# Moving the last softmax-denominator round of each head behind the V transposes' copies

## The chip, the cores and the metric

The kernel runs as one program on all 8 cores of a Trainium2 chip. Every core holds the full weights and works on its own half of the rows of one of the four batch entries, so the cores compute the same amount and exchange nothing. The metric is the device time of one launch in microseconds, that of the slowest core.

## The reference

One transformer layer with the layernorm on both sides of each block, for x of shape 4 x 2048 x 2048, in float32:

```python
def layer(x):
    x = x + _layernorm(attn(_layernorm(x)))          # 16 heads of 128, softmax over 2048 keys
    x = x + _layernorm(ffn(_layernorm(x)))           # silu(x Wg) * (x Wu), then Wd; hidden 8192
    return x

def attn(x):
    q, k, v = (x @ w_q.T), (x @ w_k.T), (x @ w_v.T)  # reshaped to heads
    p = softmax(einsum('bqhd,bkhd->bhqk', q, k) / sqrt(128))
    return einsum('bhqk,bkhd->bqhd', p, v).reshape(B, S, D) @ w_o.T
```

A core computes the attention output for 1,024 queries against all 2,048 keys, and the feed-forward block for the same 1,024 rows.

## The kernel before

The program is a list of operations for each engine, in program order, with semaphores between the engines. An engine runs its list strictly in that order; an operation whose semaphore is not there yet holds up everything behind it on that engine. The stages are A and B (layernorm, transposes, Q of all heads), C (attention, head by head), D (output projection, two layernorms), E (gate and up) and F (down, last layernorm and output).

The change lies in stage C, in the loop over the 16 heads `h` (lines 413 to 530). Of one head, scores are computed transposed: 16 chunks of 128 keys by 1,024 queries. A chunk is two matmuls into PSUM (`emit_scores_tc`, L426) and one exponential on ScalarE to bf16 (L435). The exponentials are grouped in four rounds of four chunks, which share one buffer `PTR`. Of each round two things are made:

- the product with V, 8 matmuls on TensorE that accumulate in PSUM (`emit_pv_round`, L448);
- the sum over the four chunks, on VectorE in bf16 (`emit_tree_round`): L459 and L464 add two pairs, L469 adds the sums, L477 adds that to the running denominator `RB` (L475 is a copy in its place in round 0). The last of the four operations raises `vsm`.

Between the chunks TensorE has "filler": the K and V projections of the next head in eight groups of 16 matmuls (`emit_kv_group`, L354), evacuated by ScalarE (L371). At the end of the head come the last V product, then `emit_vt`, 16 matmuls against the identity that transpose the next head's V into PSUM (L386), and `emit_vt_copies`, two VectorE copies of the result to SBUF (L398). The first score matmuls of the next head wait for these copies (`vVt`), because they write the same PSUM.

Then the denominator is summed over the partitions: two matmuls of an all-ones matrix with `RB` (L515, called the ones matmuls here), which wait for `vsm` at 4h + 4. VectorE takes the reciprocal of their result (L523, raises `vRc`) and multiplies the head's output with it (L527, raises `vO`). The ones matmuls write the PSUM banks that the K groups use. So the first filler group of a head waits for the reciprocal of the head before:

```python
            if h >= 2 and g < 2:
                w("t", vRc, h - 1)      # h here is the head whose K is projected
```

In the loop over heads that means: in heads 1 to 14, TensorE issues score chunks 0 and 1 and then waits for the reciprocal of the previous head before filler group 0. Head 15 has no filler; its first V product (L448) waits for `vO` of head 14.

The order in VectorE's list around the end of head h, before the change, is: round 3 of the sum (four operations), copy 0, copy 1, reciprocal, multiplication. In TensorE's list it is: V product of round 3, the 16 transposes, the wait for `vsm`, the two ones matmuls, scores 0 and 1 of the next head, filler 0. In ScalarE's list the first exponential of the next head also waits for `vsm` at 4h + 4, since it overwrites `PTR`.

Of the kernel before, what the change touches and what calls it, by code (L numbers as in the profile page):

```python
# [77 lines left out]
def build_nc():  # L78
# [23 lines left out]
    def Bv(off, dims, parts=128):  # L102
        return bass.AP(ABF, off, [[ABF_N, parts]] + [list(d) for d in dims])
# [4 lines left out]
    def Pv(off, dims, parts=128):  # L108
        return bass.AP(PS, off, [[4096, parts]] + [list(d) for d in dims])
# [58 lines left out]
    def op(e, f, ride=None):  # L168
        pair = None
        if ride is not None:  # L170
            c, k = ride
            c.n += k
            pair = (c.s, k)
        if pair is None:
            ops[e].append(f)
        else:
            def g(eng, f=f, pair=pair):
                f(eng).then_inc(*pair)
            ops[e].append(g)

    def w(e, c, v=None):
        if v is None:
            c, v = c
        ops[e].append(lambda eng, s=c.s, v=v: eng.wait_ge(s, v))
# [191 lines left out]
    def emit_vt(h):  # L376
        for r in range(2):
            w("t", kv_evac[("V", h, 2 * r + 1)])
            if r == 0 and h == 0:
                w("t", vA, 16)  # L380
            if r == 0 and h >= 1:
                w("t", sE, 16 * h)
            for i in range(8):
                tcv = r * 8 + i
                ride = (tVt, 1) if i == 7 else None
                op("t", lambda e, tcv=tcv, r=r, i=i: e.matmul(  # L386
                    Pv(r * 1024 + i * 128, [(1, 128)]),
                    Bv(VFM + tcv * 128, [(1, 128)]),
                    Bv(IDENT, [(1, 128)]),
                    start=True, stop=True), ride)  # L390
            vt_mm[(h, r)] = (tVt, tVt.n)

    def emit_vt_copies(h):
        for r in range(2):
            w("v", vt_mm[(h, r)])
            if h >= 1 and r == 0:
                w("v", tRd, 4 * h)
            op("v", lambda e, r=r: e.tensor_copy(  # L398
                Bv(VTM + r * 1024, [(1, 1024)]),
                Pv(r * 1024, [(1, 1024)])), (vVt, 1))  # L400
# [12 lines left out]
    for h in range(H):  # L413

        def emit_scores_tc(tc, h=h):
            pair = tc % 2
            if tc == 0:
                w("t", kv_evac[("K", h, 3)])
                w("t", vVt, 2 * h + 1)
            elif tc == 1:  # L420
                w("t", vVt, 2 * h + 2)
            else:
                w("t", sE, 16 * h + tc - 1)
            for half in range(2):
                ride = (tS, 1) if half == 1 else None
                op("t", lambda e, tc=tc, half=half, pair=pair, h=h: e.matmul(  # L426
                    Pv(pair * 1024 + half * 512, [(1, 512)]),
                    Bv(KSB + (h % 2) * 2048 + tc * 128, [(1, 128)]),
                    Bv(QF + h * 1024 + half * 512, [(1, 512)]),
                    start=True, stop=True), ride)  # L430
            r = tc // 4
            w("s", tS, 16 * h + tc + 1)
            w("s", tRd, 4 * h + r)
            w("s", vsm, 4 * h + r)
            op("s", lambda e, tc=tc, pair=pair: e.activation(  # L435
                Bv(PTR + (tc % 4) * 1024, [(1, 1024)]),
                Pv(pair * 1024, [(1, 1024)]),
                AF.Exp, bias=Fv(ST + 41, [(1, 1)]), scale=QK), (sE, 1))

        def emit_pv_round(r, h=h):  # L440
            w("t", sE, 16 * h + 4 * (r + 1))
            if r == 0:
                w("t", vO, h)
            for i in range(4):
                tcv = 4 * r + i
                for half in range(2):
                    ride = (tRd, 1) if (i == 3 and half == 1) else None
                    op("t", lambda e, tcv=tcv, i=i, half=half, r=r: e.matmul(  # L448
                        Pv(3072 + half * 512, [(1, 512)]),
                        Bv(VTM + tcv * 128, [(1, 128)]),  # L450
                        Bv(PTR + i * 1024 + half * 512, [(1, 512)]),
                        start=(r == 0 and i == 0), stop=(r == 3 and i == 3)), ride)

        def emit_tree_round(r, h=h):
            w("v", sE, 16 * h + 4 * (r + 1))
            with_lp = "bf16 softmax denominator tree (rvr impact <1e-5)"
            def t1f(e):
                with nc.allow_low_precision(with_lp):
                    return e.tensor_tensor(Bv(WDA, [(1, 1024)]),  # L459
                                           Bv(PTR, [(1, 1024)]),  # L460
                                           Bv(PTR + 1024, [(1, 1024)]), ALU.add)
            def t2f(e):
                with nc.allow_low_precision(with_lp):
                    return e.tensor_tensor(Bv(WDA + 1024, [(1, 1024)]),  # L464
                                           Bv(PTR + 2048, [(1, 1024)]),
                                           Bv(PTR + 3072, [(1, 1024)]), ALU.add)
            def t3f(e):
                with nc.allow_low_precision(with_lp):
                    return e.tensor_tensor(Bv(WDA, [(1, 1024)]),  # L469
                                           Bv(WDA, [(1, 1024)]),  # L470
                                           Bv(WDA + 1024, [(1, 1024)]), ALU.add)
            def accf(e, r=r):
                with nc.allow_low_precision(with_lp):
                    if r == 0:
                        return e.tensor_copy(Bv(RB, [(1, 1024)]),  # L475
                                             Bv(WDA, [(1, 1024)]))
                    return e.tensor_tensor(Bv(RB, [(1, 1024)]),  # L477
                                           Bv(RB, [(1, 1024)]),
                                           Bv(WDA, [(1, 1024)]), ALU.add)
            op("v", t1f, (vI, 1))  # L480
            op("v", t2f, (vI, 1))
            w("v", vI, vI.n)
            op("v", t3f, (vI, 1))
            w("v", vI, vI.n)
            op("v", accf, (vsm, 1))

        def emit_filler(h, idx):
            if h + 1 >= H:
                return
            kind = "K" if idx < 4 else "V"  # L490
            emit_kv_group(kind, h + 1, idx % 4)
            emit_kv_evac(kind, h + 1, idx % 4)

        for r in range(4):
            emit_scores_tc(4 * r)
            emit_scores_tc(4 * r + 1)
            if r >= 1:
                emit_pv_round(r - 1)
            emit_filler(h, 2 * r)
            emit_scores_tc(4 * r + 2)  # L500
            emit_scores_tc(4 * r + 3)
            emit_filler(h, 2 * r + 1)
            emit_tree_round(r)
        emit_pv_round(3)
        if h + 2 < H:
            emit_wkv(h + 2)
        if h + 1 < H:
            emit_vt(h + 1)
            emit_vt_copies(h + 1)
        w("t", vsm, 4 * h + 4)  # L510
        if h + 1 < H:
            w("t", kv_evac[("V", h + 1, 3)])
# [419 lines left out]
```

How the kernel before makes its waits and increments, by code:

```python
            def g(eng, f=f, pair=pair):  # L177
                f(eng).then_inc(*pair)
# [2 lines left out]
    def w(e, c, v=None):  # L181
        if v is None:
            c, v = c
        ops[e].append(lambda eng, s=c.s, v=v: eng.wait_ge(s, v))
```

## Time and profile before

| | us |
|---|---|
| median of 2 runs | 2683.85 (2682.86 to 2684.85) |
| profiled execution, device time | 2683.04 |
| profiled execution, span of its slowest core (core 0) | 2681.5 |
| spans of the 8 cores | 2671.3 to 2681.5 |
| TensorE busy in the span | 2321.0 (87%) |
| VectorE busy | 648.8 (24%) |
| ScalarE busy | 588.3 (22%) |

The page gives the busy time of each engine, the chain of work that ended last, and the costliest groups of instructions. Stage C runs from about 225 us to 1047 us of the span. The share of the whole span says little about an edit in it: the idle time of TensorE inside stage C, and what releases it, is what is to be read. The clock column of the windows view is the clock that TensorE was granted, as a share of its full 2.4 GHz: 1.00 is 2.4 GHz and 0.50 is 1.2 GHz.

### The profile page before, as it was taken

The page shows a single profiled execution, that of the slowest core. Times are in us where ns is not written, and L with a number is a line of the kernel's source. Part 1 is how long each engine was busy: PE and PEld are TensorE (multiplying, and loading weights), DVE is VectorE, ACT ScalarE, POOL GpSimd, SP SyncE. Part 2 cuts the span into 40 slices and gives each one's busy share as a digit, 9 for nine tenths or more (in the row PEclk, how much of TensorE's full clock was granted, in tenths as well). Part 3 has the DMA queues.
Part 4 walks back from the last instruction along what each step waited for, and adds up shares of the span by engine and source line. Part 5 has one row for each costly group of instructions (what it writes and reads, how often), then busy time and mean ns, then how long its engine had stood idle before and what let it go on. Part 6 is the DMA issues. An engine that isn't in the chain of part 4 may idle for free.

```text
span 2681.5 us, 26781 instructions; the slowest of 8 cores (2671.3 to 2681.5 us)
## 1 busy us (share of the span) xinstructions
PE 2321.0 (87%) x10701; PEld 1057.3 (39%) x10912; DVE 648.8 (24%) x760; ACT 588.3 (22%) x677; POOL 157.7 (6%) x269
## 2 busy tenths in 40 slices
PE   1999788888878886777999999999999999999950
PEld 1444334334333432333444444444444444444420
DVE  5511433433343344554000000000000001011020
ACT  5514344434434442220000000000000001011021
POOL 0000000000000000000000000000000010100001
PEclk9999899989989998887999999999999999999985
DMA  6551101101010107333444444444444454544589
GB/s 181 143 109 25 24 16 24 24 16 24 16 24 16 24 10 116 94 110 71 79 74 76 79 77 74 78 79 73 77 74 81 66 77 72 73 71 71 78 126 157
DMA packets 67624, 186.35 MB, mean 69 GB/s; under 512 B 4912, under 2 KB 37680, under 8 KB 62256
## 3 DMA queue, kind: packets, MB, share of 16 engines
q0 software_dynamic: 64048, 159.47, 35.9%
q1 hardware_dynamic: 3456, 25.17, 3.1%
q8 instruction: 89, 1.46, 0.2%
q14 instruction: 31, 0.25, 0.0%
HBM read 302.12 MB, written 25.17 MB: 122 GB/s over the span
## 4 chain that ended last, share of the span: by engine, by line
PE 79%; DVE 10%; DMA 4%; issue 2%; another core or an unknown queue 2%; ACT 1%; DVEq 0%; POOL 0%; ACTq 0%; POOLq 0%
PE ps L354 18%; PE ps L651 16%; PE ps L663 16%; PE ps L710 16%; PE ps L448 4%; PE ps L307 4%; DVE afp L523 4%; PE ps L426 4%; DMA x2s<-afp 2%; DVE afp L194 1%; DMA out<-afp 1%; DVE abf L398 1%; DVE afp L580 1%; DVE afp L588 1%
## 5 line engine op out<-in xcount | busy, mean ns | idle before, releaser
L354 PE MATMUL ps<-abf 128*128 128x512 bf16 x2020 | 485.1, 395 | 85.0 <-DVE afp L523 82.2
L710 PE MATMUL ps<-abf 128*128 128x512 bf16 x2007 | 447.8, 383 | 16.8 <-DVE abf L734 8.6
L651 PE MATMUL ps<-abf 128*128 128x512 bf16 x2007 | 452.0, 380 | 5.7 <-DVE abf L631 3.6
L663 PE MATMUL ps<-abf 128*128 128x512 bf16 x2007 | 449.8, 379 | 2.2
L354 PEld LDWEIGHTS ps<-abf 128*128 128x128 bf16 x2048 | 205.7, 101 | 349.2 <-issue 126.8
L435 ACT ACTIVATE abf<-ps,afp 128x1024 bf16<-128x1024 f32 x256 | 272.7, 1111 | 165.3 <-PE ps L448 107.3
L710 PEld LDWEIGHTS ps<-abf 128*128 128x128 bf16 x2048 | 201.3, 99 | 263.3 <-issue 28.0
L651 PEld LDWEIGHTS ps<-abf 128*128 128x128 bf16 x2048 | 200.8, 98 | 246.7 <-issue 6.4
L663 PEld LDWEIGHTS ps<-abf 128*128 128x128 bf16 x2048 | 200.5, 98 | 241.5
L679 DVE TENSOR_TENSOR abf<-afp,ps 128x1024 bf16<-128x1024 f32 x64 | 78.2, 1222 | 809.9 <-PE ps L663 809.9
L674 ACT ACTIVATE afp<-ps 128x1024 f32<-128x1024 f32 x64 | 65.5, 1024 | 804.3 <-PE ps L651 804.3
L426 PE MATMUL ps<-abf 128*128 128x512 bf16 x510 | 137.2, 384 | 27.1 <-DVE abf L398 19.3
L459 DVE TENSOR_TENSOR abf<-abf 128x1024 bf16<-128x1024 bf16 x64 | 44.3, 692 | 463.8 <-ACT abf L435 463.8
L563 PE MATMUL ps<-abf 128*128 128x512 bf16 x502 | 121.5, 404 | 37.8 <-DVE abf L603 28.9
L371 ACT ACTIVATE abf<-ps 128x512 bf16<-128x512 f32 x128 | 76.4, 597 | 324.7 <-PE ps L354 324.7
L448 PE MATMUL ps<-abf 128*128 128x512 bf16 x489 | 122.5, 386 | 5.8 <-DVE abf L527 3.1
L307 PE MATMUL ps<-abf 128*128 128x512 bf16 x499 | 113.4, 385 | 3.7 <-DVE abf L266 3.0
L734 DVE CAST abf<-ps 128x512 bf16<-128x512 f32 x16 | 9.9, 682 | 438.5 <-PE ps L710 438.5
L717 ACT ACTIVATE abf<-ps 128x512 bf16<-128x512 f32 x16 | 8.3, 602 | 444.5 <-PE ps L710 444.5
L523 DVE RECIPROCAL afp<-ps 128x1024 f32<-128x1024 f32 x16 | 104.8, 6548 | 0.9 <-PE ps L515 0.9
L563 PEld LDWEIGHTS ps<-abf 128*128 128x128 bf16 x512 | 52.3, 103 | 107.1 <-issue 54.6
L426 PEld LDWEIGHTS ps<-abf 128*128 128x128 bf16 x512 | 47.0, 98 | 99.6 <-issue 50.0
(78 smaller groups left out, 970.5 us busy)
## 6 DMA issues: line engine op xcount, KB each, us to landing
abf<-wg POOLq DMA_DIRECT2D x64, 512.0 KB, 5.1
abf<-wu POOLq DMA_DIRECT2D x64, 512.0 KB, 5.1
abf<-wd POOLq DMA_DIRECT2D x64, 512.0 KB, 5.5
afp<-xb SPq DMA_DIRECT2D x24, 1024.0 KB, 6.5
abf<-wq POOLq DMA_DIRECT2D x16, 512.0 KB, 7.2
abf<-wk POOLq DMA_DIRECT2D x16, 512.0 KB, 6.1
abf<-wv POOLq DMA_DIRECT2D x16, 512.0 KB, 6.0
abf<-wo POOLq DMA_DIRECT2D x4, 2048.0 KB, 35.5
```

Source lines behind the costliest of these rows:

```text
L307: op("t", lambda e, slot=slot, kc=kc, half=half, pair=pair: e.matmul(Pv(2048 + pair * 1024 + half * 512, [(1, 512)]), Bv(W3 + slot * 2048 ...
L354: op("t", lambda e, slot=slot, kc=kc, g=g, bank=bank: e.matmul(Pv(bank * 512, [(1, 512)]), Bv(W3 + slot * 2048 + kc * 128, [(1, 128)]), Bv ...
L371: op("s", lambda e, g=g, dst=dst, bank=bank: e.activation(Bv(dst + g * 512, [(1, 512)]), Pv(bank * 512, [(1, 512)]), AF.Copy), (sKV, 1))
L426: op("t", lambda e, tc=tc, half=half, pair=pair, h=h: e.matmul(Pv(pair * 1024 + half * 512, [(1, 512)]), Bv(KSB + (h % 2) * 2048 + tc * 12 ...
L435: op("s", lambda e, tc=tc, pair=pair: e.activation(Bv(PTR + (tc % 4) * 1024, [(1, 1024)]), Pv(pair * 1024, [(1, 1024)]), AF.Exp, bias=Fv(S ...
L448: op("t", lambda e, tcv=tcv, i=i, half=half, r=r: e.matmul(Pv(3072 + half * 512, [(1, 512)]), Bv(VTM + tcv * 128, [(1, 128)]), Bv(PTR + i ...
L523: op("v", lambda e: e.reciprocal(Fv(T1, [(1, 1024)]), Pv(2048, [(1, 1024)])), (vRc, 1))
L563: op("t", lambda e, kc=kc, j=j, qc=qc, pair=pair: e.matmul(Pv(pair * 2048 + j * 512, [(1, 512)]), Bv(OFM + kc * 1024 + qc * 128, [(1, 128) ...
L651: op("t", lambda e, slot=slot_g, kc=kc, half=half, gb=gb: e.matmul(Pv(gb * 512 + half * 512, [(1, 512)]), Bv(W3 + slot * 2048 + kc * 128, ...
L663: op("t", lambda e, slot=slot_u, kc=kc, half=half, ub=ub: e.matmul(Pv(ub * 512 + half * 512, [(1, 512)]), Bv(W3 + slot * 2048 + kc * 128, ...
L679: op("v", lambda e, hc=hc, ub=ub: e.tensor_tensor(Bv(GMAP[hc], [(1, 1024)]), Fv(T1, [(1, 1024)]), Pv(ub * 512, [(1, 1024)]), ALU.mult), (v ...
L710: op("t", lambda e, hc=hc, qc=qc, i=i, base=base, j=j: e.matmul(Pv(qc * 512, [(1, 512)]), Bv(GMAP[hc] + qc * 128, [(1, 128)]), Bv(base + i ...
```

## The change

The call that emits round 3 of the sum is taken out of the loop over rounds and is made after the copies of the transposed V. Rounds 0 to 2 stay where they were. Nothing is added or removed: VectorE's list of head h becomes copy 0, copy 1, round 3 of the sum (four operations), reciprocal, multiplication. The lists of TensorE, ScalarE and the DMA queues keep their order, and every wait keeps its value. For head 15, which has no transposes and copies, the lists stay as they were.

```diff
@@ -500,13 +500,15 @@
             emit_scores_tc(4 * r + 2)
             emit_scores_tc(4 * r + 3)
             emit_filler(h, 2 * r + 1)
-            emit_tree_round(r)
+            if r < 3:
+                emit_tree_round(r)
         emit_pv_round(3)
         if h + 2 < H:
             emit_wkv(h + 2)
         if h + 1 < H:
             emit_vt(h + 1)
             emit_vt_copies(h + 1)
+        emit_tree_round(3)
         w("t", vsm, 4 * h + 4)
         if h + 1 < H:
             w("t", kv_evac[("V", h + 1, 3)])
```

## Rows read from the trace of the kernel before

**Rows 1.** The page: costliest groups; busy us, mean ns | idle before, releaser
```profile
L354 PE MATMUL ps<-abf 128*128 128x512 bf16 x2020 | 485.1, 395 | 85.0 <-DVE afp L523 82.2
L523 DVE RECIPROCAL afp<-ps 128x1024 f32<-128x1024 f32 x16 | 104.8, 6548 | 0.9 <-PE ps L515 0.9
```
**Rows 2.** Waits of TensorE and VectorE: us in total, times, longest us
```profile
PE ps L354 <- DVE afp L523: 82.2, 14, 5.9
PE ps L426 <- DVE abf L398: 19.3, 32, 0.8
DVE abf L398 <- PE ps L386: 89.3, 16, 75.6
```
**Rows 3.** Timeline, VectorE at the end of head 9: start us, us, operation
```profile
736.25 0.69 DVE L459 TENSOR_TENSOR abf<-abf 128x1024 bf16<-128x1024 bf16 x1 [7.48 <-ACT abf L435]
736.86 0.68 DVE L464 TENSOR_TENSOR abf<-abf 128x1024 bf16<-128x1024 bf16 x1
737.65 0.69 DVE L469 TENSOR_TENSOR abf<-abf 128x1024 bf16<-128x1024 bf16 x1
738.44 0.69 DVE L477 TENSOR_TENSOR abf<-abf 128x1024 bf16<-128x1024 bf16 x1
740.05 2.35 DVE L398 CAST abf<-ps 128x1024 bf16<-128x1024 f32 x2 [0.92 <-PE ps L386]
742.32 6.55 DVE L523 RECIPROCAL afp<-ps 128x1024 f32<-128x1024 f32 x1
```
**Rows 4.** Timeline, all engines, same stretch: TensorE's work and the exponentials
```profile
739.27 1.06 PE L386 MATMUL ps<-abf 128*128 128x128 bf16 x16
...
740.38 0.38 PE L515 MATMUL ps<-abf 128*128 128x512 bf16 x1
...
742.22 2.24 ACT L435 ACTIVATE abf<-ps,afp 128x1024 bf16<-128x1024 f32 x2 [3.82 <-PE ps L426]
...
742.55 0.59 PE L426 MATMUL ps<-abf 128*128 128x512 bf16 x2 [0.54 <-DVE abf L398]
...
749.02 5.47 PE L354 MATMUL ps<-abf 128*128 128x512 bf16 x16 [5.87 <-DVE afp L523]
```
**Rows 5.** The end of head 15, the order without copies between: timeline
```profile
1037.24 0.69 DVE L477 TENSOR_TENSOR abf<-abf 128x1024 bf16<-128x1024 bf16 x1
...
1038.08 0.59 PE L515 MATMUL ps<-abf 128*128 128x512 bf16 x2 [1.10 <-DVE abf L477]
...
1038.85 6.56 DVE L523 RECIPROCAL afp<-ps 128x1024 f32<-128x1024 f32 x1 [0.91 <-PE ps L515]
```
**Rows 6.** Timeline, the first filler groups of two other heads, and a later group
```profile
644.19 4.98 PE L354 MATMUL ps<-abf 128*128 128x512 bf16 x16 [5.87 <-DVE afp L523]
...
695.88 6.43 PE L354 MATMUL ps<-abf 128*128 128x512 bf16 x16 [5.87 <-DVE afp L523]
...
713.37 3.62 PE L354 MATMUL ps<-abf 128*128 128x512 bf16 x16
```
**Rows 7.** Windows, head 9 to 10: length, busy (count) by engine, then granted clock
```profile
742.50:745.90 3.40, 0.59 (x2) 0.13 (x2) 3.40 (x1) 1.95 (x2) 0.00 (x0) 1.00 0.37 74
746.10:749.00 2.90, 0.00 (x0) 0.01 (x1) 2.80 (x2) 0.00 (x0) 0.00 (x0) 0.50 0.00 0
749.00:752.70 3.70, 3.68 (x9) 1.34 (x10) 1.20 (x1) 0.00 (x0) 0.00 (x0) 0.50 0.00 0
752.90:756.00 3.10, 3.10 (x16) 1.38 (x15) 0.00 (x0) 1.42 (x2) 0.00 (x0) 1.00 0.02 5
```
**Rows 8.** Groups of TensorE by shape in 749.0 to 752.3, then in 754.5 to 758
```profile
L354 PE MATMUL ps<-abf 128*128 128x512 bf16 x8 | 3.6, 628 | 5.9 <-DVE afp L523 5.9
...
L354 PE MATMUL ps<-abf 128*128 128x512 bf16 x14 | 3.2, 379 | 0.0
```
**Rows 9.** Timeline: two weight loads in a row of the half-clock stretch
```profile
749.40 0.15 PEld L354 LDWEIGHTS ps<-abf 128*128 128x128 bf16 x1 [0.27 <-issue]
749.82 0.15 PEld L354 LDWEIGHTS ps<-abf 128*128 128x128 bf16 x1 [0.28 <-issue]
```
**Rows 10.** Timeline, VectorE: the reciprocals of heads 0, 8 and 14
```profile
271.66 6.55 DVE L523 RECIPROCAL afp<-ps 128x1024 f32<-128x1024 f32 x1
...
689.19 6.55 DVE L523 RECIPROCAL afp<-ps 128x1024 f32<-128x1024 f32 x1
...
1003.21 6.55 DVE L523 RECIPROCAL afp<-ps 128x1024 f32<-128x1024 f32 x1
```
**Rows 11.** Timeline, start of head 15: last exponentials before the V product, and its wait
```profile
1003.11 4.30 ACT L435 ACTIVATE abf<-ps,afp 128x1024 bf16<-128x1024 f32 x4 [3.82 <-PE ps L426]
...
1011.23 2.64 PE L448 MATMUL ps<-abf 128*128 128x512 bf16 x8 [3.09 <-DVE abf L527]
```

## Prediction

> **What bounds the kernel now.** I read the page's groups first. TensorE is busy 87% of the span, so only its idle time in stage C can be at stake. One releaser stands out there: the filler matmuls of L354 sat idle for 82.2 us, released by the reciprocal of L523 [rows 1]. The view of waits says how that is spread: 14 times, never more than 5.9 us [rows 2]. Those are heads 1 to 14, where filler 0 waits for `vRc` of the previous head. So at each head's end VectorE is on the path: whatever delays the reciprocal delays TensorE by the same amount. Then I read the timeline of one head's end. VectorE finishes round 3 of the sum at 738.44 + 0.69 = 739.13 us, sits idle for 0.92 us until the first transposes are done, copies from 740.05 us, and starts the reciprocal at 742.32 us [rows 3]. TensorE ran the ones matmuls at 740.38 us, inside the copies, since `vsm` had come before them [rows 4]. Their 6.5 us reciprocal follows the copies without a gap.
>
> Is this one head or all? The waits for the transposes add up to 89.3 us in 16 times, the longest 75.6 us [rows 2]; that one is the first copy of the stage. The rest is 89.3 - 75.6 = 13.7 us over 15 heads, 0.91 us each. Every head has the gap of 0.92 us, so in every head the sum is already finished when the copies could start.
>
> **What the change does, step by step.**
>
> 1. Round 3 leaves the place before the copies. Gain: nothing. The copies wait for TensorE's transposes there, with 0.92 us to spare [rows 3], and the transposes wait for nothing that VectorE gives. I exclude a gain for this reason.
>
> 2. Round 3 now stands between copy 1 and the reciprocal. In front of it is work that ends 2.27 us after the first copy starts (742.32 - 740.05) [rows 3]. From the start of its first operation to the start of its last it takes 738.44 - 736.25 = 2.19 us [rows 3].
>
> 3. The ones matmuls wait for `vsm`, and now nothing covers them: TensorE stands at that wait, with the next head's scores queued behind it, and VectorE has only the reciprocal behind the sum, which needs their result. Head 15 shows this order in the kernel before: L477 starts at 1037.24 us, the ones matmuls at 1038.08 us, the reciprocal at 1038.85 us, that is 1.61 us from the start of L477 to the start of the reciprocal [rows 5].
>
> The reciprocal thus starts 2.27 + 2.19 + 1.61 = 6.07 us after the first copy instead of 2.27 us. It is late by 3.80 us.
>
> 4. What is late next. Filler 0 in heads 1 to 14 follows the reciprocal, 14 times 3.80 us. In head 15 the first V product waited 3.09 us for the multiplication after head 14's reciprocal [rows 11], so it shifts too. That is 15 x 3.80 = 57.0 us. The scores 0 and 1 of the next head also come later, behind the ones matmuls, and their exponentials after them, 2.24 us for two [rows 4]. They have the whole reciprocal of 6.55 us as cover. The first exponential's own wait for `vsm` is met before the scores are. Without this cover they would cost 1.2 us of matmul pairs and 2.24 us a head. In head 15 four exponentials, 4.30 us [rows 11], lie under the reciprocal and the multiplication, 7.8 us together. The weight transfers wait for matmuls that shift as a whole, and cost nothing.
>
> 5. TensorE's clock. After the last scores, which end at 743.14 us, the granted clock is still 1.00 up to 745.9 us and 0.50 (1.2 GHz) from 746.1 us; filler 0 then starts at half clock, and only from 752.9 us is it 1.00 again [rows 7]. A matmul shows 628 ns at the half clock and 379 ns at the full one [rows 8], and two start 0.42 us apart [rows 9] against 3.62 / 16, at most 0.23 us [rows 6]. In the changed kernel TensorE idles from 740.33 us, where the transposes end, to about 740.05 + 2.27 + 2.88 + 0.15 = 745.35 us, 5.0 us, before the ones matmuls. (2.88 us is the whole round, 739.13 - 736.25.) The clock fell 3 us after the last matmul in the row above. So I expect it to be at 1.2 GHz for the ones matmuls in most heads. That adds 0.25 us for a longer matmul and 0.21 us for the later start of the second, 0.46 us a head on the path. Bounds: never, 0; always, 15 x 0.46 = 6.9 us. I take three heads in four, 5 us.
>
> 6. Filler 0 itself. It ran at half clock for part of its time before, too: 4.98, 6.43 and 5.47 us in three heads, against 3.62 us at full clock [rows 4, 6]. So the loss was 1.36 to 2.81 us a head. Its mean comes from the period of the heads. From head 8's to head 9's reciprocal it is 742.32 - 689.19 = 53.13 us [rows 3, 10] with a loss of 2.81 us, so 50.32 us without any. The mean period is (1003.21 - 271.66) / 14 = 52.25 us [rows 10], so the mean loss is 1.93 us. The change shifts when the filler starts against the changes of the clock. I can't tell the new pattern; the bounds are all heads at 1.36 us, 14 x -0.57 = -8 us, and all at 2.81 us, 14 x 0.88 = +12 us. The middle of what was seen is 2.09 us, which makes 14 x 0.16 = +2 us.
>
> The Trainium skill, "TensorE: Matmul & The Clock Gate" (Part 1: The HAM clock gate), advises against fitting such a count at all: it puts the ramp penalty below 1% of a typical kernel span. By it steps 5 and 6 drop out and the sum is 57 us instead of 64. The trace is not against the rule as to size, since 14 x 1.93 = 27 us is 1% of the span, but here seven microseconds decide on which side of 2% the result falls.
>
> **The sum.** 57.0 + 5 + 2 = 64 us. Against the profiled execution's own time, 2683.04 + 64 = 2747.0 us (span 2745.5 us). That execution is 0.8 us below the median of the runs shown, which is less than anything else in the sum. Nothing behind stage C changes; I add nothing for it.
>
> **The rivals.**
>
> *The clock gives back.* The mechanism is the one above and filler 0 lands well: with ones matmuls at full clock and every filler at the shortest loss the sum is 57 - 8 = 49 us, 2732 us; with both neutral it is 57 us, 2740 us. For it: shorter losses of 1.36 us do occur [rows 6]. Against it: a longer pause before the ones matmuls speaks for more half clock, not less. 2% of the time is 53.7 us, about what a measurement of this kernel can tell from no change. It falls within 2% only if steps 5 and 6 together give back over 3.3 us. Chance 0.16, of which 0.08 falls below 2%.
>
> *The clock costs more.* All ones matmuls slow, all fillers at 6.43 us, and head 15, whose short matmul groups are all on the path, some 3 us slower: 57 + 7 + 12 + 3 = 79 us, 2762 us. For it: three different losses in a row show that the pattern is not fixed. Against it: no two of the three neighbours I looked at had the worst value. Chance 0.13 for the upper part, over 2756 us.
>
> *Copies freed: faster.* If VectorE were still summing when the transposes end, round 3 would hold up the copies, the copies would hold up the scores (19.3 us of waits for them, in 32 times [rows 2]), and putting them first would bring that time back: at most the 2.88 us of a round in 15 heads, 43 us, for 2640 us. It decides where the gap before the copies is zero; it takes over as soon as the transposes end more than 0.92 us earlier. Against it: the gap is there in every head [rows 2], and the reciprocal would have to come after the sum in any case. Chance 0.01.
>
> *Nothing moves.* If the wait for `vsm` was bound by something else that ends after 745.2 us, or the sum fitted an idle stretch of VectorE, the time would stay at 2683 us. VectorE's only idle time between the copies and the end of the multiplication is none [rows 3], so this needs a wait I have not seen. Chance 0.03.
>
> **How the numbers follow.** The forecast, 57 us plus a clock cost between 0 and some 16 us, has the remaining 0.67; 57 + 5 + 2 is its middle. The range of 2736 to 2758 us leaves out the two rivals that change nothing or gain, the lower half of the giving back, and most of the costly clock: 0.04 + 0.06 + 0.10 = 0.20. Slower by over 2% (above 2737.5 us): 0.67 + 0.13 + 0.08 = 0.88. Within 2%: 0.08 + 0.03 = 0.11. Faster: 0.01.
>
> **What would show each step right or wrong.** Step 1: the gap before the copies is now longer than 0.92 us, by about the 2.88 us of the round, and the copies start as soon after the transposes as before. Steps 2 and 3: L477 ends just before the ones matmuls in all 16 heads, TensorE shows a wait of about 5 us for L477 in 15 heads (75 us in all), and the reciprocal starts 6.1 to 6.5 us after the first copy. Step 4: the wait of filler 0 for the reciprocal is still there, 14 times and about 6 us; the waits of the scores for the copies are gone; the head period is 52.25 + 4.3 = 56.5 us. Steps 5 and 6: the granted clock is 0.50 at the ones matmuls in most heads, and filler 0 takes 5 to 6.5 us. What would make it wrong: the ones matmuls starting before L477 ends, filler 0 following something else than L523, or a clock that stays at 1.00 over the pause.

## The result and the profile after

The changed kernel takes 2751.8 us against 2684.9 us for the kernel before in the same comparison: a ratio of 1.025, 95% interval 1.0238 to 1.0261. It is slower by 67 us (2751.83 - 2684.91). In some executions the cores of one half of the chip, or of both, show a lower clock and the time is longer; the ratios leave these out. The forecast was 2747 us with a range of 2736 to 2758 us.

The page of the changed kernel gives the span of its slowest core:

```profile
span 2746.7 us, 26992 instructions; the slowest of 8 cores (2740.3 to 2746.7 us)
PE 2359.4 (86%) x10912; PEld 1064.7 (39%) x10912; DVE 648.8 (24%) x760; ACT 586.7 (21%) x677; POOL 157.7 (6%) x269
```

VectorE is busy for 648.8 us, as before: no work was added. The difference is in the waits. These are those of TensorE and VectorE after (us in total, times, longest us):

```profile
PE ps L517 <- DVE abf L477: 77.1, 16, 5.1
PE ps L354 <- DVE afp L525: 72.3, 14, 5.2
...
DVE abf L398 <- PE ps L386: 244.1, 16, 75.6
...
DVE afp L525 <- PE ps L517: 22.6, 16, 1.4
```

The first line is the new wait. TensorE stands in front of the ones matmuls (now L517) until the last addition of round 3 is done, about 5.1 us in each of heads 0 to 14 and 0.2 us in head 15, whose order is that of before. The wait of filler 0 for the reciprocal [rows 1, 2] is still there 14 times, since the reciprocal (now L525) is as long as it was. It fell from 5.9 to 5.2 us only because scores 0 and 1 now run during the reciprocal. Of the 19.3 us in which scores waited for the copies [rows 2], 1.0 us is left.

The end of head 9 in the timeline, to be held against [rows 3] and [rows 4]. Each line has the start, the duration, engine, line and operation, and in brackets the idle time before it.

```profile
780.25 1.06 PE L386 MATMUL ps<-abf 128*128 128x128 bf16 x16
781.04 2.36 DVE L398 CAST abf<-ps 128x1024 bf16<-128x1024 f32 x2 [11.28 <-PE ps L386]
783.31 0.68 DVE L459 TENSOR_TENSOR abf<-abf 128x1024 bf16<-128x1024 bf16 x1
...
785.49 0.69 DVE L477 TENSOR_TENSOR abf<-abf 128x1024 bf16<-128x1024 bf16 x1
786.43 0.94 PE L517 MATMUL ps<-abf 128*128 128x512 bf16 x2 [5.13 <-DVE abf L477]
787.16 1.91 PE L426 MATMUL ps<-abf 128*128 128x512 bf16 x4
787.55 6.56 DVE L525 RECIPROCAL afp<-ps 128x1024 f32<-128x1024 f32 x1 [1.36 <-PE ps L517]
```

From the first copy to the reciprocal it is now 787.55 - 781.04 = 6.51 us, where it was 2.27 us. The copies start no earlier after the transposes (0.79 us after their start, 0.78 us before). The gap in front of them is 11.28 us instead of 0.92 us: it now holds the 2.88 us of round 3 that left, and the 7.48 us that VectorE used to wait for round 3's exponentials [rows 3].

The granted clock around the pause (windows view: stretch, its length, busy time and count of PE, PEld, DVE, ACT, POOL, then the clock, the DMA share and GB/s):

```profile
783.50:786.30 2.80, 0.00 (x0) 0.00 (x0) 2.48 (x4) 0.00 (x0) 0.00 (x0) 1.00 0.15 28
786.40:788.00 1.60, 1.56 (x4) 0.58 (x5) 0.45 (x1) 0.00 (x0) 0.00 (x0) 0.55 0.00 0
788.00:794.00 6.00, 1.08 (x3) 0.15 (x1) 6.00 (x1) 2.12 (x2) 0.00 (x0) 0.50 0.00 0
794.20:799.50 5.30, 5.25 (x13) 1.90 (x14) 1.23 (x1) 0.00 (x0) 0.00 (x0) 0.50 0.01 3
800.00:801.00 1.00, 1.00 (x5) 0.41 (x4) 0.00 (x0) 0.11 (x1) 0.00 (x0) 0.90 0.00 0
```

It is still 1.00 during the idle stretch and near 0.50, that is 1.2 GHz, just as the ones matmuls run. And it stays there through the reciprocal and into filler 0, which is slow for at least its first 5.3 us; from 800 us on the clock is back (0.90 over that microsecond).

### The profile page after: what moved, and what is told of

It is laid out like the page before. It is cut to its first block, busy times and chain, and to the rows that moved or that the text cites. A ratio compares the mean times of both kernels' runs of the same rounds, so it can differ in the third digit from the quotient of the medians.

```text
span 2746.7 us, 26992 instructions; the slowest of 8 cores (2740.3 to 2746.7 us)
## 1 busy us (share of the span) xinstructions
PE 2359.4 (86%) x10912; PEld 1064.7 (39%) x10912; DVE 648.8 (24%) x760; ACT 586.7 (21%) x677; POOL 157.7 (6%) x269
## 4 chain that ended last, share of the span: by engine, by line
PE 78%; DVE 11%; DMA 4%; issue 3%; another core or an unknown queue 2%; ACT 1%; DVEq 0%; POOL 0%; ACTq 0%; POOLq 0%
PE ps L354 17%; PE ps L653 16%; PE ps L665 16%; PE ps L712 15%; PE ps L307 4%; PE ps L448 4%; DVE afp L525 4%; PE ps L426 3%; DMA x2s<-afp 2%; DVE afp L194 1%; DMA out<-afp 1%; DVE abf L398 1%; DVE afp L582 1%; DVE afp L590 1%
## 5 line engine op out<-in xcount | busy, mean ns | idle before, releaser
L354 PE MATMUL ps<-abf 128*128 128x512 bf16 x2048 | 492.9, 397 | 73.6 <-DVE afp L525 72.3
L712 PE MATMUL ps<-abf 128*128 128x512 bf16 x2048 | 449.8, 383 | 13.8 <-DVE abf L736 8.6
L653 PE MATMUL ps<-abf 128*128 128x512 bf16 x2048 | 454.6, 380 | 3.2 <-DVE abf L633 3.2
L665 PE MATMUL ps<-abf 128*128 128x512 bf16 x2048 | 452.5, 379 | 0.0
L354 PEld LDWEIGHTS ps<-abf 128*128 128x128 bf16 x2048 | 206.6, 101 | 348.4 <-issue 128.1
L712 PEld LDWEIGHTS ps<-abf 128*128 128x128 bf16 x2048 | 201.3, 99 | 262.3 <-issue 26.6
L653 PEld LDWEIGHTS ps<-abf 128*128 128x128 bf16 x2048 | 200.7, 98 | 246.5 <-issue 6.2
L665 PEld LDWEIGHTS ps<-abf 128*128 128x128 bf16 x2048 | 200.5, 98 | 241.5
L676 ACT ACTIVATE afp<-ps 128x1024 f32<-128x1024 f32 x64 | 65.5, 1024 | 804.3 <-PE ps L653 804.3
L426 PE MATMUL ps<-abf 128*128 128x512 bf16 x512 | 148.4, 414 | 9.4 <-ACT abf L435 8.4
L565 PE MATMUL ps<-abf 128*128 128x512 bf16 x512 | 127.5, 416 | 31.0 <-DVE abf L605 22.7
L448 PE MATMUL ps<-abf 128*128 128x512 bf16 x512 | 124.3, 387 | 2.9 <-ACT abf L435 1.5
L307 PE MATMUL ps<-abf 128*128 128x512 bf16 x512 | 114.2, 384 | 2.7 <-DVE abf L266 2.7
L525 DVE RECIPROCAL afp<-ps 128x1024 f32<-128x1024 f32 x16 | 104.9, 6557 | 22.6 <-PE ps L517 22.6
L398 DVE CAST abf<-ps 128x1024 bf16<-128x1024 f32 x32 | 37.7, 1219 | 244.1 <-PE ps L386 244.1
L565 PEld LDWEIGHTS ps<-abf 128*128 128x128 bf16 x512 | 53.3, 105 | 105.7 <-issue 56.0
```

Source lines behind the costliest of these rows:

```text
L307: op("t", lambda e, slot=slot, kc=kc, half=half, pair=pair: e.matmul(Pv(2048 + pair * 1024 + half * 512, [(1, 512)]), Bv(W3 + slot * 2048 ...
L354: op("t", lambda e, slot=slot, kc=kc, g=g, bank=bank: e.matmul(Pv(bank * 512, [(1, 512)]), Bv(W3 + slot * 2048 + kc * 128, [(1, 128)]), Bv ...
L448: op("t", lambda e, tcv=tcv, i=i, half=half, r=r: e.matmul(Pv(3072 + half * 512, [(1, 512)]), Bv(VTM + tcv * 128, [(1, 128)]), Bv(PTR + i ...
L525: op("v", lambda e: e.reciprocal(Fv(T1, [(1, 1024)]), Pv(2048, [(1, 1024)])), (vRc, 1))
L565: op("t", lambda e, kc=kc, j=j, qc=qc, pair=pair: e.matmul(Pv(pair * 2048 + j * 512, [(1, 512)]), Bv(OFM + kc * 1024 + qc * 128, [(1, 128) ...
L653: op("t", lambda e, slot=slot_g, kc=kc, half=half, gb=gb: e.matmul(Pv(gb * 512 + half * 512, [(1, 512)]), Bv(W3 + slot * 2048 + kc * 128, ...
```

## The experiments

Three theories are set against each other. The path theory is that of the prediction: what counts is how late the reciprocal starts, because filler 0 waits for it. The score theory is a rival formed after the result: the ones matmuls hold up scores 0 and 1 of the next head, and through them the exponentials, and it is these that cost. The clock theory says that most of the loss is TensorE's half clock after the long pause. The edits are shown abridged, partly in words; "..." stands for lines left out.

### Only the last addition behind the copies

```diff
-            emit_tree_round(r)
+            emit_tree_round(r, "sums" if r == 3 else None)    # L459, L464, L469
...
             emit_vt_copies(h + 1)
+        emit_tree_round(3, "acc")                             # L477 alone
```

> Only the last of the four additions of round 3 stands behind the copies; the other three are where they were before. Path theory (what counts is how late the reciprocal of each head starts): in the rows of the kernel before, the reciprocal starts 2.27 us after the first copy, and L477 to reciprocal is 1.61 us, so it is 1.61 us late, 15 x 1.61 = 24 us, 2709 us; the pause of TensorE is 2.9 us long instead of 5.0, so the ones matmuls should mostly run at the full clock (if not, up to 7 us more). Clock theory (most of the loss is TensorE's half clock after the long pause, little of it the round itself): the pause is now under 3 us, the loss vanishes, 2690 us or less. Score theory (the late scores 0 and 1 and their exponentials are what costs): they are some 2.1 us later than before, 15 x 2.1 = 32 us, 2716 us.

Measured: a ratio of 1.0116 (1.0095 to 1.0138), the profiled execution at 2716.4 us; 31 us slower than before. In its timeline (VectorE) most heads look like this, with 3.97 us from copy to reciprocal, against 3.88 us expected:

```profile
597.32 2.36 DVE L398 CAST abf<-ps 128x1024 bf16<-128x1024 f32 x2 [1.71 <-PE ps L386]
601.29 6.56 DVE L526 RECIPROCAL afp<-ps 128x1024 f32<-128x1024 f32 x1 [1.02 <-PE ps L518]
```

The total is that of the score theory (2716 us), but the sum was made of other parts. The reciprocal is 1.78 us later on the mean of heads 0 to 14, a little more than the path theory has it: about 1.70 us in the twelve heads with ones matmuls at the full clock, where 1.61 us was expected, and 2.12 us in the three with slow ones. The rest is filler 0, which takes 6.11 us on the mean instead of 5.54 us. The clock theory falls here: with a pause under 3 us the loss should have gone. This run alone does not tell path and scores apart.

### Round 3 between copy 0 and copy 1

```diff
             op("v", ... tensor_copy(VTM + r * 1024 <- PSUM r * 1024) ..., (vVt, 1))
+            if r == 0:
+                emit_tree_round(3)      # of head h, while the V of h + 1 is copied
```

> Round 3 stands between copy 0 and copy 1, so that copy 1 covers the ones matmuls again. Path theory: the reciprocal is late by the round alone, 2.8 us, and not by the 0.99 us at full clock or 1.4 us at half clock that the ones matmuls take uncovered: 15 x 2.8 = 42 us, 2727 us, with 8 us either way for the clock at filler 0. If the ones matmuls aren't a part of the loss, the time is that of the changed kernel, 2752 us. Score theory: scores 1 wait for copy 1 as before and come 2.8 us late too, 42 us, the same number; this run does not tell those two apart.

Measured: 1.0132 (1.011 to 1.0154), the profiled execution at 2719.6 us, 35 us slower, where 42 us, give or take 8, were expected. With copy 1 over the ones matmuls the kernel is well below the changed one, so their time, uncovered, is a part of the loss. In heads where they run at the full clock the reciprocal starts 604.16 - 599.10 = 5.06 us after copy 0, that is 2.8 us late, as expected. The timeline shows a head of either sort; others lie between them, with the second of the ones matmuls slower than the first:

```profile
543.54 1.23 DVE L398 CAST abf<-ps 128x1024 bf16<-128x1024 f32 x1 [11.28 <-PE ps L386]
547.48 1.22 DVE L398 CAST abf<-ps 128x1024 bf16<-128x1024 f32 x1
549.00 6.56 DVE L528 RECIPROCAL afp<-ps 128x1024 f32<-128x1024 f32 x1 [0.30 <-PE ps L520]
599.10 1.23 DVE L398 CAST abf<-ps 128x1024 bf16<-128x1024 f32 x1 [11.28 <-PE ps L386]
603.03 1.22 DVE L398 CAST abf<-ps 128x1024 bf16<-128x1024 f32 x1
604.16 6.55 DVE L528 RECIPROCAL afp<-ps 128x1024 f32<-128x1024 f32 x1
```

In the first of the two the ones matmuls end after copy 1, and the reciprocal waits 0.30 us for them.

### Extra matmuls in the pause

```diff
+        for i in range(20):                  # ahead of the wait for vsm, heads 0 to 14
+            matmul(PSUM 2048 + (i % 2) * 512, ONESC, QF + (i % 2) * 512)
         w("t", vsm, 4 * h + 4)
```

> The changed kernel, with 20 additional matmuls (about 4.3 us at the full clock) in TensorE's pause between the transposes and the ones matmuls; their result is overwritten. They tell what the half clock costs at the ones matmuls. Path theory with the clock term of the prediction: the ones matmuls run at full clock, the reciprocal starts 0.46 us earlier, 15 x 0.46 = 7 us less than the changed kernel, about 2745 us, with a few us either way for filler 0, which still follows an idle stretch of over 5 us. Clock theory: filler 0 starts at the full clock too and the time falls by 7 + 14 x 2.2 = 38 us to 2714 us. If the half clock costs nothing there, 2752 us.

Measured: 1.021 (1.0192 to 1.0228), median 2740.9 us. The ones matmuls of the changed kernel and of this one (one line's instructions: durations in ns, minimum, median, maximum, first and last start):

```profile
L517 PE MATMUL ps<-abf x32: 502/608/634, 274.8 to 1106.5; 128*128 128x512 bf16 x32
```
```profile
L523 PE MATMUL ps<-abf x32: 376/377/378, 273.9 to 1098.2; 128*128 128x512 bf16 x32
```

All 32 were slow in the changed kernel and all 32 run at the full clock here. The reciprocal starts 6.06 us after the first copy in head after head:

```profile
831.78 2.36 DVE L398 CAST abf<-ps 128x1024 bf16<-128x1024 f32 x2 [11.28 <-PE ps L386]
...
837.84 6.56 DVE L531 RECIPROCAL afp<-ps 128x1024 f32<-128x1024 f32 x1 [0.91 <-PE ps L523]
```

That is the 6.07 us that the prediction put together for full-clock ones matmuls. In the changed kernel it is 6.56 us on the mean of 15 heads, so the half clock costs 0.50 us a head there, 7.5 us in all. Filler 0 is no faster for it: 5.81 us on the mean against 5.84 us. The gain in the whole is somewhat more: 10.9 us between the medians, 8.3 us between the profiled executions. On the mean of the eight cores the last reciprocal comes 7.1 us earlier and the span is 9.1 us shorter, so the rest lies behind stage C; what makes it there was not looked into.

### Scores 0 and 1 ahead of the ones matmuls

```diff
         emit_tree_round(3)
+        emit_scores_tc(0, h + 1)             # no longer at the start of head h + 1
+        emit_scores_tc(1, h + 1)
         w("t", vsm, 4 * h + 4)
```

> The changed kernel, but TensorE issues scores 0 and 1 of the next head ahead of the ones matmuls, as soon as the copies are done. The scores then run as early as in the kernel before; the exponentials still wait for round 3, since they overwrite its input, and the reciprocal is as late as in the changed kernel. Score theory (the late score matmuls cost): the loss falls to that of the exponentials, under 15 us, 2700 us or less. Path theory: the reciprocal still starts 3.8 us late at least, 57 us; the pause before the ones matmuls is 2.5 us instead of 5.0, which may spare up to 7 us: 2741 to 2752 us.

Measured: 1.0247 (1.0229 to 1.0266), against 1.025 (1.0228 to 1.0272) for the changed kernel beside it: no difference. The timeline shows scores 1 right behind copy 1, as in the kernel before. The reciprocal starts 6.17 us after the first copy in this head, where the ones matmuls ran at the full clock, and 6.46 us after it on the mean, nearly as late as in the changed kernel (6.56 us):

```profile
778.89 2.36 DVE L398 CAST abf<-ps 128x1024 bf16<-128x1024 f32 x2 [11.28 <-PE ps L386]
...
781.39 0.59 PE L426 MATMUL ps<-abf 128*128 128x512 bf16 x2 [0.54 <-DVE abf L398]
...
784.13 2.12 ACT L435 ACTIVATE abf<-ps,afp 128x1024 bf16<-128x1024 f32 x2 [6.90 <-DVE abf L477]
...
785.06 6.56 DVE L529 RECIPROCAL afp<-ps 128x1024 f32<-128x1024 f32 x1 [1.02 <-PE ps L521]
...
791.76 5.25 PE L354 MATMUL ps<-abf 128*128 128x512 bf16 x16 [6.88 <-DVE afp L529]
```

The score theory falls. Scores nearly 5 us earlier and exponentials some 2 us earlier are worth nothing, because filler 0 still follows the reciprocal; its wait only grows to 6.88 us.

### The changed kernel again

> The changed kernel itself, on the same chip as the two runs above, so that they can be set against it: 2752 us, with the ones matmuls at the half clock in all or nearly all heads and filler 0 at 5 to 6.5 us.

It ran beside the kernel above and the last one below. Measured: 1.025 (1.0228 to 1.0272), median 2751.2 us. The head period is 56.82 us against 56.85 us, and the ones matmuls are slow in heads 0 to 14 as in the first run; in head 15 they ran at the full clock this time.

### Taking the reciprocal off TensorE's path

```diff
-                w("t", vRc, h - 1)                  # K groups wait for the reciprocal
+                w("t", sRe, h - 1)                  # ... for ScalarE's copy
...
+        op("s", activation(T1 + 1024 <- PSUM 2048, AF.Copy), (sRe, 1))
+        w("v", sRe, h + 1)
-            Fv(T1, ...), Pv(2048, ...)              # reciprocal reads PSUM
+            Fv(T1, ...), Fv(T1 + 1024, ...)         # reads the copy in SBUF
```

> The kernel before (sum ahead of the copies), but ScalarE copies the result of the ones matmuls from PSUM to SBUF, the K groups wait for this copy instead of the reciprocal, and the reciprocal reads the SBUF copy. The reciprocal is as long and starts as late as before, but nothing on TensorE waits for it until the first V product. Path theory: the 14 waits of 5.87 us go, and with them the half clock at filler 0, 14 x (5.87 + 1.93) = 109 us, 2576 us; less gain if the first V product now waits for the multiplication. If the reciprocal isn't what TensorE's time hangs on, the wait turns up elsewhere and the time stays near 2685 us.

Measured, in the order of the kernel before: 0.9581 (0.9564 to 0.9598), median 2572.7 us, 112 us faster. The timeline around the end of a head:

```profile
623.97 2.35 DVE L399 CAST abf<-ps 128x1024 bf16<-128x1024 f32 x2 [0.92 <-PE ps L387]
...
624.08 0.59 PE L516 MATMUL ps<-abf 128*128 128x512 bf16 x2
624.83 1.02 ACT L524 ACTIVATE afp<-ps 128x1024 f32<-128x1024 f32 x1 [2.51 <-PE ps L516]
...
626.24 6.54 DVE L530 RECIPROCAL afp<-afp 128x1024 f32<-128x1024 f32 x1
626.47 0.59 PE L427 MATMUL ps<-abf 128*128 128x512 bf16 x2 [0.54 <-DVE abf L399]
626.90 3.62 PE L355 MATMUL ps<-abf 128*128 128x512 bf16 x16
```

The reciprocal starts 2.27 us after the first copy and takes 6.54 us, as before, yet filler 0 starts right behind scores 1 and takes 3.62 us: no wait and no half clock. The head period is 44.29 us instead of 52.25 us. That is 7.96 us a head, where 5.87 + 1.93 = 7.80 us were expected.

### The same, in the changed order

> The order of the changed kernel together with the freed banks (ScalarE copies the result of the ones matmuls, filler 0 waits for that copy). If only the reciprocal's lateness costs anything, the change of order is free here, since nothing on TensorE waits for the reciprocal any more: 2573 us, as with the freed banks alone. Path theory: TensorE's own pause in front of the ones matmuls remains. They start some 5.3 us after the first copy, are slow (0.77 + 0.46 us), the copy takes about 1 us, and filler 0 starts 7.3 us after the first copy instead of about 2.9 us: 4.4 us in 15 heads, 66 us, and 1 to 2.8 us a head more if the pause now brings filler 0 to the half clock: 2640 to 2680 us.

Measured: 0.9916 (0.99 to 0.9931), median 2660.8 us, inside the 2640 to 2680 us of the path theory. Compared with 2572.7 us for the freed banks alone, the change of order costs 88 us, more than in the kernel it was made for. (The two have their own executions of the kernel before beside them, with medians of 2683.8 and 2684.2 us.) The reciprocal can't be what makes it dear here: no filler waits for it any more, and only the first V product of head 15 waits for the multiplication behind it, 2.6 us with the changed order and 3.1 us without. TensorE waits 78.3 us in 16 times for the last addition of round 3, and that alone is enough. The timeline shows the pause, now in front of work that would otherwise start at once:

```profile
772.42 2.35 DVE L399 CAST abf<-ps 128x1024 bf16<-128x1024 f32 x2 [11.28 <-PE ps L387]
...
777.82 1.01 PE L518 MATMUL ps<-abf 128*128 128x512 bf16 x2 [5.13 <-DVE abf L478]
778.62 1.91 PE L427 MATMUL ps<-abf 128*128 128x512 bf16 x4
778.98 1.02 ACT L526 ACTIVATE afp<-ps 128x1024 f32<-128x1024 f32 x1 [8.22 <-PE ps L518]
...
780.33 5.07 PE L355 MATMUL ps<-abf 128*128 128x512 bf16 x16
```

Filler 0 starts 780.33 - 772.42 = 7.91 us after the first copy, against 626.90 - 623.97 = 2.93 us. That is 4.98 us later, and in this head it takes 1.45 us longer, since the pause brings in the half clock that the freed banks had taken away. The head periods say the same over all heads: 50.32 - 44.29 = 6.0 us, and 15 times that is 90 us.

### All runs in one table

The head period is the distance from the first to the fifteenth reciprocal, divided by 14; the other columns are means from the timelines, over heads 0 to 14 for the reciprocal and over the 14 fillers 0. All are read on the slowest core.

| kernel | first copy to reciprocal | filler 0 | head period | period less before's |
|---|---|---|---|---|
| before | 2.27 | 5.54 | 52.25 | |
| last addition behind | 4.05 | 6.11 | 54.62 | 2.37 |
| round 3 between the copies | 5.23 | 5.34 | 55.03 | 2.78 |
| changed, pause filled | 6.06 | 5.81 | 56.32 | 4.07 |
| changed, scores first | 6.46 | 5.78 | 56.69 | 4.44 |
| changed | 6.56 | 5.84 | 56.85 | 4.60 |
| changed, again | 6.56 | 5.81 | 56.82 | 4.57 |
| freed banks | 2.27 | 3.62 | 44.29 | -7.96 |
| freed banks, changed order | 7.77 | 4.64 | 50.32 | -1.93 |

In the first six rows under "before", where filler 0 waits for the reciprocal, the last column is the sum of the changes in the first two, to within 0.05 us: 4.29 + 0.30 = 4.59 for the changed kernel, 2.96 - 0.20 = 2.76 for the round between the copies. So nothing else in a head changed its length by more than that.

## Why the prediction was right

Its premise, that each head's end hangs on VectorE's reciprocal, held in every run that left that wait in place. Steps 2 to 4 gave 57.0 us from 15 times 3.80 us. The run with the filled pause has 6.06 - 2.27 = 3.79 us.

Step 5 had the size right (0.46 us expected, 0.50 us measured) and the number of heads too low: the ones matmuls were slow in all 16 heads of the changed kernel, not in three of four. That makes 15 x (6.56 - 6.07) = 7.4 us instead of 5 us. Step 6 took +2 us for filler 0, and it was 14 x 0.30 = 4 us. Both of these were choices inside bounds, and the prediction says of the second that it can't tell the new pattern: that each came out within 2.4 us of its size is in part luck. The three terms with their measured sizes are 57.0 + 7.4 + 4.1 = 68.5 us. The last reciprocal of stage C started at 1107.35 us instead of 1038.85 us, 68.5 us later. That sets core 1, the slowest after, against core 0, the slowest before, and the spans of these two differ by 65.2 us only. Stage C ends at somewhat different times on different cores: on the mean of all eight the last reciprocal comes 65.9 us later (1106.0 instead of 1040.1 us), and the span is 66.2 us longer. So nearly the whole loss arises in stage C, and the forecast of 64 us was short of it by 2 to 3 us.

The Trainium skill, "TensorE: Matmul & The Clock Gate" (Part 1: The HAM clock gate), advises against fitting a count of slow matmuls, because the ramp penalty is under 1% of a typical kernel span. In this case the pauses recur in every head and the whole penalty is not under 1%: 14 x 1.93 = 27 us, 1.0% of the span, in the kernel before, and 14 x (5.84 - 3.62) + 7.4 = 38 us, 1.4%, in the changed one. The change moved it by 11.5 us. Without steps 5 and 6 the forecast would have been 2683.04 + 57 = 2740.0 us, 12 us below what was measured.

The prediction also calls 2% about what a measurement of this kernel can tell from no change. It can tell far less: the 95% interval of the ratio is 1.0238 to 1.0261, about 0.1% to either side.

Of the rivals, "the clock gives back" and "the clock costs more" were the right place to look and had the wrong size: only the second direction occurred, at 11.5 us of its 22 us. "Copies freed" is excluded by the copies, which start as soon after the transposes as before, and "nothing moves" by the 77.1 us that TensorE now waits for L477.

Three details of what the profile would show were off. The gap before the copies did not grow by 2.88 us but by 10.36 us: I had counted the work that left and forgotten that VectorE's wait for the exponentials in front of it merges with the gap. The wait of filler 0 for the reciprocal became 5.2 us instead of about 6 us, since the scores moved into it. And the head period is 56.85 us, not 56.5 us.

## What to carry to other kernels

- When work is moved back on an engine that seems idle (VectorE is busy 24% here), look for who waits for it next: 2.88 us of additions cost 4.6 us a head, because the two matmuls that read the result lost their cover too, and then their clock.
- A wait of the busiest engine for a slow operation can be a wait for a buffer. Here a copy of 1.02 us on an engine that was free at that moment let go of two PSUM banks that a 6.55 us reciprocal had held, and the kernel's time fell by 4.2%, while every other order of the additions that was run made it longer.
- The same reordering costs more in the better kernel (88 us against 67 us), where TensorE otherwise has no long wait at the end of a head.

## What the runs showed of the hardware

The full-size reciprocal takes 6.55 us for 128 x 1024 float32 elements from PSUM [rows 3] and 6.54 us from SBUF, so reading PSUM is not what makes it slow; two copies out of PSUM, with as many elements each, take 2.36 us together.

The granted clock did not follow one length of pause. In the kernel before it fell 3 us after the last matmul [rows 7]; in the changed kernel it stood at 1.00 almost to the end of a pause of 5.1 us and was at half clock for the matmuls behind it. With the last addition behind the copies the pause is 2.9 us; the ones matmuls ran at the full clock in twelve of the heads 0 to 14 and slowly in heads 3, 8 and 13. In head 3 the last transpose ended at 433.7 us and the clock had fallen 2.1 us later at the latest:

```profile
432.30:435.60 3.30, 1.41 (x19) 1.00 (x17) 2.16 (x2) 0.00 (x0) 0.00 (x0) 1.00 0.42 67
435.80:436.60 0.80, 0.00 (x0) 0.00 (x0) 0.59 (x1) 0.00 (x0) 0.00 (x0) 0.50 1.06 210
```

With scores first the last part of the pause is 2.3 us long, and the ones matmuls are at the full clock in heads 4, 9 and 14 and slow, one or both of them, in the rest of heads 0 to 14. And filling one pause with 20 matmuls left filler 0, behind the next pause, as slow as it was.

The differences between the heads of one kernel are not random; after the first few they come round in a fixed order. Filler 0 takes 5.47, 4.98 and 6.43 us in turn in the kernel before, 6.02, 6.54 and 5.08 us in the changed one, and 6.37 and 5.25 us in turn with the filled pause. What sets this order was not settled by these runs.
